# Sixteen small products in bfloat16 in place of float32: the token list of a mixture-of-experts layer on one Trainium2 core

## The reference, cut to what matters

```
def _moe(x, ln_w, ln_b, router_w, expert_wv, expert_proj):
    h = _layernorm(x, ln_w, ln_b)
    logits = h @ router_w
    expert_idx = jnp.argmax(logits, axis=-1)
    ...
    for e in range(E):
        gv = h @ expert_wv[e]
        gate_raw, value = jnp.split(gv, 2, axis=-1)
        y = gate_raw * jax.nn.sigmoid(gate_raw) * value @ expert_proj[e]
        out = out + jnp.where((expert_idx == e)[..., None], y, 0.0)
```

## Time and profile before

| | |
|---|---|
| median of 3 runs | 2651.42 us (2646.68 to 2652.11) |
| the profiled execution | 2654.03 us, of which the span is 2652.2 us |
| PE busy over the span | 2257.2 us (85%) |
| the 32 passes of the 16 products (L2537) | start at 2171.5, end 7.0 us later |
| first large product of the experts (L2546) | starts at 2184.3 |

### The profile page before, as it was taken

The page is one execution under the profiler, slowest core; times in us unless marked ns, Lnnn a source line. Parts: engine busy times, 40 slices in busy tenths (PEclk is TensorE's granted clock), DMA queues, the critical chain, the costliest instruction groups (busy, mean ns, idle before and its releaser), DMA issues. The chain is left out here.

```text
span 2652.2 us, 38396 instructions
## 1 busy us (share of the span) xinstructions
PE 2257.2 (85%) x12302; PEld 1165.0 (44%) x12303; DVE 1974.4 (74%) x1868; ACT 1819.6 (69%) x2842; POOL 1328.6 (50%) x508
## 2 busy tenths in 40 slices
PE   7788888888888888888888897779978979999988
PEld 2344444444434444444444352323422255665547
DVE  6899999999978999999999458782384142225665
ACT  5899999999959999999999335207604731113256
POOL 2099998999942999989999212000000022110020
PEclk8899999999999999999999979879988979999999
DMA  2510001000015000010000012001000051001000
GB/s 91 139 44 28 28 28 40 28 28 27 24 74 135 29 26 25 28 41 27 28 28 21 18 48 84 1 1 38 28 1 25 25 231 69 24 22 38 0 10 32
DMA packets 57112, 110.27 MB, mean 42 GB/s; under 512 B 13123, under 2 KB 18499, under 8 KB 55984
## 3 DMA queue, kind: packets, MB, share of 16 engines
q1 hardware_dynamic: 48656, 97.58, 11.7%
q0 software_dynamic: 8352, 11.31, 1.5%
HBM read 84.97 MB, written 23.59 MB: 41 GB/s over the span
## 5 line engine op out<-in xcount | busy, mean ns | idle before, releaser
L1522 POOL TENSOR_TENSOR hs<-hs,c_bc 128x2048 f32<-128x2048 f32 x256 | 1166.7, 4557 | 60.5 <-DVE hs L1573 45.0
L1573 DVE TENSOR_TENSOR_SCAN hs<-decays,ps 128x512 f32<-128x512 f32 x512 | 610.9, 1216 | 28.8 <-ACT decays L1536 10.0
L1573 DVE TENSOR_TENSOR_SCAN hs<-decays,carry,ps 128x512 f32<-128x512 f32 x512 | 621.5, 1269 | 5.7 <-PE ps L1600 4.7
L1608 PE MATMUL ps<-hs,sel 128*64 128x512 f32 x2048 | 496.3, 605 | 16.7 <-POOL hs L1522 16.4
L1600 PE MATMUL ps<-ident,dbu_even 128*128 128x128 f32 x2048 | 296.3, 283 | 97.5 <-DVE hs L1573 64.1
L1600 PE MATMUL ps<-ident,dbu_odd 128*128 128x128 f32 x2048 | 294.8, 283 | 92.4 <-DVE hs L1573 61.5
L1536 ACT ACTIVATE decays<-delta_far,A 128x512 f32<-128x512 f32 x512 | 359.3, 715 | 7.3 <-DVE hs L1573 7.2
L1536 ACT ACTIVATE decays<-delta_near,A 128x512 f32<-128x512 f32 x512 | 360.2, 716 | 1.8 <-DVE hs L1573 1.8
L1544 ACT ACTIVATE dbu_odd<-du_turned,b_turned 128x512 f32<-128x512 f32 x512 | 359.5, 715 | 0.0
L1544 ACT ACTIVATE dbu_even<-du_turned,b_turned 128x512 f32<-128x512 f32 x496 | 348.4, 715 | 0.0
L1600 PEld LDWEIGHTS ps<-ident,dbu_even 128*128 128x128 f32 x2048 | 220.1, 142 | 248.1 <-DVE hs L1573 192.9
(11 more groups left out here) (338 smaller groups left out, 2623.4 us busy)
## 6 DMA issues: line engine op xcount, KB each, us to landing
c_bc<-c_rows SPq DMA_DIRECT2D x256, 128.0 KB, 2.9
o_rows<-osb SPq DMA_DIRECT2D x26, 256.0 KB
u_rows<-u SPq DMA_DIRECT2D x4, 1024.0 KB, 4.5
d_rows<-delta SPq DMA_DIRECT2D x4, 1024.0 KB, 4.2
delta_near<-d_rows SPq DMA_DIRECT2D x4, 1024.0 KB, 10.1
hs<-u_rows SPq DMA_DIRECT2D x4, 1024.0 KB, 6.7
delta_far<-d_rows SPq DMA_DIRECT2D x4, 1024.0 KB, 12.9
w_down<-in_expert_proj SPq DMA_DIRECT2D x1, 4096.0 KB, 31.8
```

The source lines that it names most:

```text
L1522: pool.tensor_tensor(x, x, spread(c_bc[:, g, :], 4), ALU.mult).then_inc(weighed.sem, 1)
L1573: dve.tensor_tensor_scan(hs[:, quad % RING, n, :], decays[:, s % RING, :], ps[:, DBU + s % RING, :], carry[:, at(i * GB, g), blk] if q els ...
L1608: mm = pe.matmul(ps[lo:lo + DB, ACC + quad % 2 * 2 + j // 2, :], k.sel2[:, :], hs[:, quad % RING, j, :], start=False, stop=False, skip_gro ...
```

## The change

`lands` and `id_in_tile` become bfloat16, so that each of the 16 products is one of bfloat16 matrices. The token's number (1 to 2048) doesn't fit bfloat16, so it is split into two parts that do: 128 times the number of its group, and 1 to 128. The two parts stand side by side, so `id_in_tile` is 128 x 38 for each group: columns 0 to 18 the first part, 19 to 37 the second. The 0/1 matrix `in_tile` that was written over before is now a float32 tile of its own, and a third large DVE operation is added in front of `lands` to make the second part. The last of the three small DVE operations, a cast, becomes an addition of the first part that rounds into the integers. The input `token_ids` has one column more.

```
-    id_in = k.sb("id_in_tile", [P, TT, NT], ctx=ctx)
+    in_tile = k.sb("in_tile", [P, TT, NT], ctx=ctx)
+    id_in = k.sb("id_in_tile", [P, TT, 2, NT], BF16, ctx=ctx)
...
-    lands = k.sb("lands", [P, N // P, P], ctx=ctx)
+    lands = k.sb("lands", [P, N // P, P], BF16, ctx=ctx)
...
-                    pe.wait_ge(landed.sem, landed.at(t + 3))
-                    mm = pe.matmul(ps[:, OUT, 0:NT], lands[:, t, :], id_in[:, t, :], start=(t == 0), stop=(t == TT - 1))
+                    pe.wait_ge(landed.sem, landed.at(t + 4))
+                    mm = pe.matmul(ps[:, OUT, 0:2 * NT], lands[:, t, :], id_in[:, t, :, :].rearrange("p j s -> p (j s)"),
+                                   start=(t == 0), stop=(t == TT - 1))
...
-            dve.tensor_tensor(id_in[:], each(tile_of[:], "p (t a) -> p t a", a=1),
+            dve.tensor_tensor(in_tile[:], each(tile_of[:], "p (t a) -> p t a", a=1),
                               each(numbers[:, P:P + NT], "p (a s) -> p a s", a=1), ALU.is_equal).then_inc(landed.sem, 1)
             dve.wait_ge(landed.sem, landed.at(1))
-            dve.tensor_tensor(id_in[:], id_in[:], each(ids[:, 0:TT], "p (t a) -> p t a", a=1), ALU.mult)\
+            dve.tensor_tensor(id_in[:, :, 0, :], in_tile[:], each(ids[:, 0:TT], "p (t a) -> p t a", a=1), ALU.mult)\
                .then_inc(landed.sem, 1)
+            dve.tensor_scalar(id_in[:, :, 1, :], in_tile[:], ids[:, TT:TT + 1], None, ALU.mult).then_inc(landed.sem, 1)
...
-            dve.tensor_copy(token[:], token_f[:]).then_inc(tokens_known.sem, 1)
+            dve.tensor_tensor(token[:], ps[:, OUT, 0:NT], token_f[:], ALU.add).then_inc(tokens_known.sem, 1)
```

More of the change, by code:

```diff
@@ L2254, in experts @@
         tile_of, row_of = k.sb("tile_of", [P, TT], ctx=ctx), k.sb("row_of", [P, TT], ctx=ctx)
-        ids = k.sb("token_ids", [P, TT], ctx=ctx)
+        ids = k.sb("token_ids", [P, TT + 1], ctx=ctx)
         expert = k.sb("tile_expert", [1, NT + 1], I32, ctx=ctx)
@@ L2668, in _ @@
             dve.wait_ge(ids_summed.sem, ids_summed.at(1))
-            dve.tensor_scalar(blank[:], ps[:, OUT, 0:NT], 0.0, k.empty[:, D:D + 1], ALU.is_equal, ALU.mult)\
+            dve.tensor_scalar(blank[:], ps[:, OUT, NT:2 * NT], 0.0, k.empty[:, D:D + 1], ALU.is_equal, ALU.mult)\
                .then_inc(tokens_known.sem, 1)
             dve.wait_ge(tokens_known.sem, tokens_known.at(1))
-            dve.scalar_tensor_tensor(token_f[:], ps[:, OUT, 0:NT], -1.0, blank[:], ALU.add, ALU.add)\
+            dve.scalar_tensor_tensor(token_f[:], ps[:, OUT, NT:2 * NT], -1.0, blank[:], ALU.add, ALU.add)\
                .then_inc(tokens_known.sem, 1)
             dve.wait_ge(tokens_known.sem, tokens_known.at(2))
-            dve.tensor_copy(token[:], token_f[:]).then_inc(tokens_known.sem, 1)
+            dve.tensor_tensor(token[:], ps[:, OUT, 0:NT], token_f[:], ALU.add).then_inc(tokens_known.sem, 1)
             all_tiles(dve, body)
-    landed.passed(TT + 2)
+    landed.passed(TT + 3)
     late_in.passed(16 * len(late))
@@ L3224, in lay_out @@
                                .astype(np.float32), (P, 1))
-    a["token_ids"] = (1 + np.arange(P)[:, None] + np.arange(N // P)[None, :] * P).astype(np.float32)
+    a["token_ids"] = np.concatenate([np.tile(np.arange(N // P) * P, (P, 1)), 1 + np.arange(P)[:, None]], axis=1)\
+        .astype(np.float32)
     a["no_token"] = (N + 1 + np.arange(P)[:, None]).astype(np.float32)
```

## The result

The changed kernel takes 2645.75 us in the median of 22 runs (2636.23 to 2650.37), against 2652.14 us for the kernel before (2644.91 to 2656.25) in 22 runs beside it. The ratio is 0.9973, with a 95% interval of 0.9964 to 0.9982: 7.2 us less, and 4.8 to 9.5 less by the interval (the medians differ by 6.4). The forecast was 2646.1 us, 5.3 us less, in a range from 2641.4 to 2650.2.

What follows compares the result with a forecast made beforehand. PE's 32 float32 passes alone were taken to bound the stretch from 2172.3 to 2178.5. An earlier `blank` saves 5.30 us, less 0.03 for small operations: 2651.42 - 5.3 = 2646.1 us, range 2641.4 to 2650.2.

Steps and rivals of the forecast that it cites:

- D: Time from the block's first DVE operation to the first large product; forecast 10.9 us instead of 16.1.
- Step 1: DVE ahead of the lands: one added operation of 371 ns delays them by 0.29 us, hidden for PE's start.
- the rival of slow lands: Writing bfloat16 slows the sixteen DVE lands by 1.1 us in all; saving 4.2 us, time 2647.2 us, chance 0.07.
- Step 2: DVE's lands in bfloat16: no slower to write, pitch left at 0.196 us.
- Step 3: Sixteen products on PE: 32 passes become 16 at about 0.10 us pitch, so `blank` starts 5.30 us earlier (5.2 to 5.5).
- the middle between PE and DVE: End of the sixteen products: 2173.17, between 2173.27 by PE's pitch and 2173.08 by the last `lands`.
- the signs: Expected profile: 16 products within 1.9 us, near 1.3 if they keep pace with the lands, 1.8 if weights set it.
- The rule of the Trainium skill: Non-float32 weights 128 columns wide load about twice as fast, so the lands set the products' end; saving 5.4 us.
- Step 4: Three small DVE operations behind the products: the cast becomes an addition, 0 to 0.07 us more, taken as 0.03.
- Step 5: What the earlier list triggers: stores and weights are not late; fetch, turn, copy and first product move forward as one piece.
- The clock: Clock at large products gives some back, saving 1.9 to 3.9 us, chance 0.07; or saves up to 2.45 more, chance 0.07.
- The long cold stretch of the slower rival: Large products: PE stays at 1.2 GHz for more than 15.5 us, making the kernel slower; 27 us gives 2657, chance 0.04.

Runs made afterwards that it cites:

- wide_f32: The changed kernel with float32 instead of bfloat16 matrices, still two number parts and 38 columns; ratio to the kernel before 0.9997.
- f32_first: The kernel before, with the sixteen products moved ahead of PE's four register loads; ratio to the kernel before 1.0003.
- bf16_first: The changed kernel with the sixteen products moved ahead of PE's register loads; one run without a ratio, first DVE operation to first large product 10.52 us.
- bf16_warm3: The changed kernel with three float32 products of 512 columns added on PE in the wait for the fetched rows; ratio to the kernel before 0.9976.
- bf16_warm2: The changed kernel with two float32 products of 512 columns added on PE in the wait for the fetched rows; ratio to the kernel before 0.9981.

## Why the prediction was right

The mechanism held and the saving was sized a little low; that the time came out so close is in part luck. The forecast of 2646.1 us is 0.4 us from the measured 2645.75, because two misses cancel: the kernel before came out 0.7 us slower here (2652.14 instead of 2651.42), and the medians differ by 6.4 us instead of 5.3. What follows goes by D, which was to fall by 5.3 us, to 10.9, and fell by 5.68, to 10.46.

**What bounded.** Both readings held. PE alone was the bound behind 2172.3: wide_f32 keeps the whole wait, the type takes it away. And PE's queue, not DVE, set the start of the products: f32_first moved it from 3.30 to 1.23 us.

**Step 1, one DVE operation more.** Predicted 371 ns for it and 0.29 us of delay; measured 0.37 us, and the `lands` start 2166.68 - 2166.39 = 0.29 us behind it. Hidden for PE's start as said, on the path for the last `lands` as said.

**Step 2, lands in bfloat16.** 3.22 us for the sixteen, unchanged; the rival of slow lands is out.

**Step 3, the sixteen products.** Right in kind, and its terms were the ones off. I took a pitch of 0.10 us from the row with 128 columns and then the middle between PE and DVE as the last to finish. The pitch of 38 columns is 0.033, so there was no middle to take: DVE was last by itself. And the tail from the last `lands` to `blank`, which I had at 2173.12 - 2172.57 = 0.55 us, is 0.31: the last product starts 0.07 behind the last `lands` and not 0.10, its weights add nothing in front of it where I had 0.10 (the two records start together), and a product of 38 columns lasts 0.20 us and not 0.31. `blank` came 10.35 - 4.72 = 5.63 us earlier, against 5.30 predicted and bounds of 5.2 to 5.5, so it lies outside them. The 0.33 us are 0.09 for the middle and 0.24 for the tail. The sign for the products' own time was off as well: my sum gave 2173.08 - 2171.46 = 1.6 us for products that keep pace with the lands, and not the 1.3 that I wrote under the signs; it is 1.53. Some 0.2 us of the 5.63 belong to a late start in this profile of the kernel before, which the forecast took over: PE's start is on its path, and its first register load took 0.93 us; against wide_f32, where the products start at 3.04 and `blank` at 10.12, the gain is 5.40. For the changed kernel the start doesn't count, as bf16_first shows. The rule of the Trainium skill that I had set beside the row (TensorE: Matmul & The Clock Gate, Weight-path perf modes) would have given 5.4. The traces agree with what follows from it, that the weights don't hold the products back; a shorter load they don't show, since each load's record still lasts 0.10 to 0.12 us. What I missed is that in the row of line 1743 the 128 columns, and not the weights, set the pitch of 0.10: with weights of the same size and type, 38 columns go at 0.033. That row alone could not tell the two apart.

**Step 4, the small operations.** Predicted 0.03 us more. From the start of `blank` to the end of `token_of` it is 0.67 us, after 0.66.

**Step 5, what follows.** The stores of `xs` were not late, nor were the weights: from the start of the first fetch to the first large product it is 2175.95 - 2171.72 = 4.23 us, after 4.28. The block moved as one piece, by 5.68 us.

**The clock.** The prediction left its place open by 2.4 us to one side and up to 3.4 to the other. The 3.4 is worked out from no row. The ten profiles without three added products have 8.65 to 10.16 us for the 16 passes, with float32 (9.57, 8.94, 10.16) and bfloat16 lists (9.09, 8.90, 9.07, 9.28, 8.65, 8.83, 10.06) mixed: the change moves nothing here that these runs can show. The long cold stretch of the slower rival appears in none of them. Its premise is that PE's work ahead of the large products counts for the clock. With three products of 512 columns right ahead of the rows the large products ran at the high clock in three profiles of three. With 7 us of float32 passes of few columns, followed by some 4.4 us of waiting, they started at 0.50 in three of three. The two differ in the kind of work and in the wait behind it, and no run parts them.

**The size in the time.** 5.68 us is a ratio of 0.9979 (and 5.4 us one of 0.9980). The two measured ratios, 0.9973 and 0.9970, hold it within their intervals, but both lie below it by 1.5 to 2.3 us. No profile shows where more would come from: from the end of the 16 passes to the end of the span it is 458.3 us before (2652.2 - 2168.16 - 25.71), 456.5 in the changed kernel, 458.2 in bf16_warm3 and 457.4 in bf16_first, and between 456.5 and 458.4 in all thirteen, with no order by type. I take the rest for noise of the runs, but that isn't shown.

## What to carry to other kernels

A chain between two blocks, where all engines wait for a few small operations, is worth its full length. A small float32 product with 128 x 128 weights in such a chain took as long with 19 columns as with 38, so try bfloat16 if the numbers can be split into exact parts. The columns that the split adds cost nothing in float32 here; in bfloat16 they set the pitch (0.033 us for 38, 0.10 for 128), which stayed hidden behind DVE. Find out which engine is last after each edit, because the same reordering in PE's queue was worth 2.1 us before the change, nothing behind it, and up to 0.3 once DVE was faster. And where spans vary by 10 us, measure 5 us by a distance within the profile that repeats.

## What the runs showed of the hardware that was not expected

- At clock 0.50, sixteen bfloat16 products with 128 x 128 weights and 38 columns follow each other every 0.033 us, although each load of weights shows 0.10 to 0.12 us: loads overlap. Float32 passes with weights of the same size follow every 0.21 us, with 19 columns as with 38.
- The first register load of the block took 0.52 to 1.18 us in nine executions with the same instructions ahead, and 0.49 to 0.50 in the four in which the products stood ahead of it; the three behind it 0.30 each, and some 0.65 us with their register instructions.
- Two wide products (3.4 us busy), then 2.1 us with PE busy for 0.47, and the clock was high for the gap and mostly low (0.61) for the 4 us of work behind it (bf16_warm2). Three such products, reaching up to the turning of the rows or to within 0.42 us of it, gave 0.97 to 1.00.
- Two DVE operations of 1024 elements with two tensors (2.35 us) beat sixteen of 128 with one (3.22 us), although each element takes longer in them.
